# A decoder block with a chunked recurrence: its preparation divided by token halves and spread between the bursts of the recurrence

## The chip, the cores and the metric

One core of a Trainium2 chip (trn2) runs the kernel. The time is device microseconds of one launch. Engines are named as in the profile: PE (matmul), PEld (its weight loads), DVE, ACT, POOL, SP (which issues the DMAs).

## The reference, cut to what matters

Three layers, each `x = layernorm(x + layer(x))`, on x of 16 x 64 tokens x 256 features:

```python
# 1: recurrence with a state per head (16 heads of 16), 16 sequences of 64 tokens in chunks of 16
q = silu(x @ Wq); k = normalise(x @ Wk); v = x @ Wv; beta = sigmoid(x @ Wbeta) * 2
def step(S, (qi, ki, vi, ei)):
    kh = ki @ S;  kh_hat = layernorm(kh)
    gw = (w * kh_hat + b - (vi - ki)) * w
    v_new = (gw - mean(gw) - kh_hat * mean(gw * kh_hat)) * rstd
    qh = qi @ S - (tril(qi @ ki.T) * ei) @ v_new
    o = qi + layernorm(qh) * w + b
    S = S - (ki * ei).T @ v_new
o = rmsnorm(o * sigmoid(x @ Wg1 @ Wg2)) * norm_w @ Wo
# 2: cross attention to ctx (16 x 64 x 128), 16 heads of 128, rmsnorm on q and k
# 3: feed-forward (704), input, weights w1, w2 and hidden rounded to 127 levels (quant-dequant)
```

Each of the 16 sequences has 64 tokens, so the recurrence has `NCH` = 4 chunks, and all sequences and heads go through a chunk together.

## The kernel before, in words

It is written by hand for each engine: every engine has its own list of work, in order, and semaphores between them. The order of an engine's list is all that decides what runs when.

**Preparation** is a list of `jobs`: each fills one of the eight PSUM banks in turn (job n takes bank n % 8) on PE and is emptied by ACT or DVE (`emptied_by`). In order: four jobs transpose x (`xt`); k, q, v, four jobs of four passes each (L446); beta (L453), gate (L461); transposes of ctx and of the value weights; the row scales of w1 (`s1`, through a matrix `diag`); transposes of the rounded w1; `mvo`, value weights times output weights (L501); then `s2` and `w2t`. DVE turns k and v into rows (L1115, L1126), squares and normalises k, and rounds w1 and w2 (L1087); POOL scales w1 and w2, makes `diag`, and adds and multiplies the bias and weight of the inner norm into `pR` (`p_rows`, L1459).

**Recurrence.** For each chunk c and each half h (features), PE runs three kinds of bursts of 64 small tiles: `scores_ttt(c, h)` (L554), `state_products(c, h)` (L562) and `own_terms(c, h)` (L572). DVE reads the state product and sums its squares (`state_read`), ACT takes the root, DVE works through `chain(c, h)` (L1201 to L1221) to `ub`, which `own_terms` wants, then reads the result and updates the state (`after_own_terms`, L1231 to L1239), which the next chunk's `state_products` want. The output of a chunk is normalised, gated and normalised again: ACT squares (L914, L918), DVE sums and inverts (L1244, L1248), POOL gates it in four operations (`out_gated`, L1482 to L1486) and scales it (L1490); the last chunk is done by DVE.

In the gaps between the bursts stand the 32 **key units** of the cross attention, placed by `KEY_PLACES`: a projection (L535), a square and a copy on ACT (L896, L900), and a column sum (L525). All of chunk 0's bursts come after all preparation jobs.

**Token pipeline.** From `ttt_out(0)` (L723) on, eight tiles of 128 tokens go through output projection, attention and feed-forward. It wants x again, and the four quarters of Wq of the cross attention (`xwq`), whose buffers lie over data of the recurrence: SP loads quarter 0 and x in chunk 1's time, 1 and 2 in chunk 2's, 3 after the last burst.

Of the kernel before, what the change touches and what calls it, by code (L numbers as in the profile page):

```python
# [23 lines left out]

# [11 lines left out]
P = 128  # L36
# [18 lines left out]
KEY_PLACES = [(2, 1, 2, 2, 1), (1, 2, 1, 1, 2, 1), (1, 2, 1, 1, 2, 1), (1, 2, 3, 2)]  # L55
# [3 lines left out]
def decoder_block(nc, x, ctx_in, Wq, Wk, Wv, Wo, Wbeta, ln_w, ln_b, Wg1, Wg2, norm_w,  # L59
                  XWq, XWk, XWv, XWo, gq, gk, w1_in, w2_in, out):  # L60
    stack = ExitStack()
    with stack:
# [31 lines left out]
        ctx2 = place("ctx2", B * CD)  # L94
        mvo = place("mvo", XH * D)
        w1t = place("w1t", KT * FF, BF16)
# [13 lines left out]
        xwv = place("xwv", XH * XD)  # L110
        xwo = place("xwo", XH * D)
        assert cursor[0] <= kt_at + 6 * XH * P

        cursor[0] = kt_at + 6 * XH * P
        xt = place("xt", KT * B * T)
        xwvt = place("xwvt", XH * CD)
        assert cursor[0] <= after_kt
# [8 lines left out]
        xwk = place("xwk", XH * XD)  # L126
        ctxt = place("ctxt", B * T)
        krow1 = place("krow1", BANK, over="ctxt")
        pR = place("pR", NCH * CW)
        onehot = place("onehot", 64)  # L130
        kinv = place("kinv", P)
        qbR = place("qbR", NCH * CW)
        sgR = place("sgR", NCH * CW)
        negeta = place("negeta", NCH * G)
        wR, bR, w2R = (place(n, KT * 32) for n in ("wR", "bR", "w2R"))
        nwc = place("nwc", KT * 32)
        chain_at = cursor[0]

        kR = place("kR", NCH * CW)
        tmp1 = place("tmp1", NCH * CW, over="ogt")  # L140
        wk, wq, wv = (place(n, KT * D) for n in ("wk", "wq", "wv"))
        wbeta = place("wbeta", KT * H)
        wbg = place("wbg", KT * P)
        wg1 = place("wg1", KT * DH)
        wg2 = place("wg2", D)
        bgt = place("bgt", B * T)
        ss = place("ss", NCH * G)
        sd = place("sd", NCH * G)
        diag = place("diag", NW1 * P)
        w2q = place("w2q", KT * FF // 2, BF16)  # L150
        prelim_end = cursor[0]
# [9 lines left out]
        sup = place("sup", CW)  # L161
        m12 = place("m12", 2 * G)
# [4 lines left out]
        cursor[0] = max(cursor[0], prelim_end)  # L167
# [3 lines left out]
        ksq = place("ksq", 2 * BANK)  # L171

# [80 lines left out]
        for n in range(4):  # L253
            job("xt", n, by="act" if n < 2 else "dve")
        for kind, by in (("k", "dve"), ("q", "act"), ("v", "dve")):
            for hh in range(KT):
                for half in range(2):
                    job(kind, hh, half, by=by)
        for half in range(2):
            job("beta", half, by="act")  # L260
        for hh in range(KT):
            for half in range(2):
                job("gate", hh, half, by="act")
        for n in range(2):
            job("ctxt", n, by="act")
        for n in range(4):
            job("xwvt", n, by="act")
        for n in range(3):
            job("s1", n, by="act")
        for n in range(4):  # L270
            job("w1t", n, by="act")
        for n in range(8):
            job("mvo", n, by="act")
        job("s2", 0, by="act")
        for n in range(2):
            job("w2t", n, by="act")
        index_of = {(k, key): n for n, (k, key, _) in enumerate(jobs)}

        def emptied_by(n):
            by = jobs[n][2]  # L280
            return sem("prep_" + by), sum(1 for j in jobs[:n + 1] if j[2] == by)

# [39 lines left out]
        def _(sp):  # L322
# [3 lines left out]
            def load_x():  # L326
                flat = x.rearrange("b t d -> (b t) d")
                for half in range(2):
                    load(xn[:, half * 4 * D:(half + 1) * 4 * D].rearrange("p (i d) -> p i d", d=D),
                         flat[half * 512:(half + 1) * 512, :].rearrange("(i p) d -> p i d", p=P), "x")  # L330
# [18 lines left out]
            for k in range(KT):  # L349
                load(nwc[:, k:k + 1], norm_w.rearrange("(k p o) -> k p o", p=P, o=1)[k], "nw")  # L350
# [1207 lines left out]
```

## Time and profile before

| | us |
|---|---|
| median of 3 runs | 446.63 |
| the three runs | 441.91, 446.63, 449.75 |
| profiled execution | 441.95 |
| its span, first to last instruction | 440.1 |

| engine | busy us | share of span |
|---|---|---|
| PE | 362.4 | 82% |
| DVE | 266.0 | 60% |
| ACT | 218.0 | 50% |
| POOL | 120.9 | 27% |

The busy shares are averages over stages that have different limits; the windows by stage and the chain of waits say more. The granted clock of PE over the span is 0.919 of the full 2.4 GHz; it has two levels, so this is a mix of stretches at 1.2 and at 2.4.

### The profile page before, as it was taken

Reading aid. Unit: us, or ns where it says so; the run is one execution under the profiler, and the core shown is the slowest. Engines: PE = TensorE matmul, PEld = TensorE weight load, DVE = VectorE, ACT = ScalarE, POOL = GpSimd, SP = SyncE. Lnnn points to the kernel's source line nnn. Section 1 sums busy time; section 2 is a strip of 40 time slices with the busy share of each in tenths; the row PEclk is TensorE's granted clock in tenths of the full one; section 3 lists DMA queues with packets and bytes.
Section 4 is the critical chain, followed back from the end, with each engine's and each line's share of the span. In section 5 each row is a group of like instructions: output and inputs, shape, how many; then the busy total and the mean of one; then the engine's idle time right before and its main releaser. Section 6 shows DMA issues by size and latency. Waiting matters only on the chain.

```text
span 440.1 us, 10666 instructions
## 1 busy us (share of the span) xinstructions
PE 362.4 (82%) x4506; PEld 212.4 (48%) x4506; DVE 266.0 (60%) x494; ACT 218.0 (50%) x584; POOL 120.9 (27%) x132
## 2 busy tenths in 40 slices
PE   3999979779977735596799999999999999996942
PEld 2445844435433212343465665755757557473621
DVE  1579945499996886504243384673946728367564
ACT  3035954545533333063646757468475584753320
POOL 3042891022040041103033332343223432233001
PEclk9999969988968969589899999999999999998975
DMA  8990000000323001901010010100100100000000
GB/s 260 240 365 11 1 4 5 3 4 3 81 75 101 2 0 35 211 7 48 0 41 11 1 48 12 44 6 13 49 12 25 25 14 0 12 3 0 12 0 25
DMA packets 17630, 19.93 MB, mean 45 GB/s; under 512 B 3360, under 2 KB 15024, under 8 KB 17328
## 3 DMA queue, kind: packets, MB, share of 16 engines
q1 hardware_dynamic: 17552, 19.24, 16.0%
q8 instruction: 36, 0.59, 0.6%
q14 instruction: 10, 0.08, 0.1%
q10 hardware_dynamic: 32, 0.02, 0.0%
HBM read 18.07 MB, written 1.18 MB: 44 GB/s over the span
## 4 chain that ended last, share of the span: by engine, by line
PE 50%; DVE 19%; ACT 13%; POOL 8%; issue 7%; DMA 1%; SPq 1%; POOLq 0%; DVEq 0%; ACTq 0%
PE ps L626 9%; PE ps L535 7%; PE ps L672 5%; PE ps L446 5%; PE ps L525 4%; PE ps L680 3%; PE ps L640 3%; PE ps L572 3%; POOL pr L1525 3%; POOL pr L1527 3%; PE ps L554 3%; PE ps L649 2%; DVE pr L1382 2%; DVE pr L1379 2%; DVE mx L1381 2%
## 5 line engine op out<-in xcount | busy, mean ns | idle before, releaser
L626 PE MATMUL ps<-xwq,x1t 128*128 128x512 f32 x128 | 65.0, 638 | 0.9 <-ACT x1t L997 0.9
L680 PE MATMUL ps<-mvo,cxp 128*128 128x256 f32 x256 | 58.4, 382 | 0.1
L680 PEld LDWEIGHTS ps<-mvo,cxp 128*128 128x128 f32 x256 | 47.6, 190 | 6.7 <-issue 0.4
L535 PE MATMUL ps<-ctxt,xwk 128*128 128x512 f32 x64 | 39.0, 716 | 2.4 <-issue 2.2
L975 ACT ACTIVATE qjunk<-ps 128x128 f32<-128x128 f32 x128 | 33.5, 280 | 9.9 <-PE ps L626 9.7
L896 ACT ACTIVATE ksq<-ps 128x512 f32<-128x512 f32 x32 | 19.0, 594 | 38.3 <-PE ps L525 28.2
L626 PEld LDWEIGHTS ps<-xwq,x1t 128*128 128x128 f32 x128 | 24.0, 202 | 27.5 <-issue 24.7
L985 ACT ACTIVATE qt<-ps 128x512 f32<-128x512 f32 x32 | 19.2, 601 | 23.4 <-PE ps L640 23.3
L525 PE MATMUL ps<-ksq,onehot 128*32 128x512 f32 x64 | 21.8, 680 | 9.2 <-ACT ksq L896 9.1
L672 PE MATMUL ps<-pt,ctx 64*128 64x512 f32 x64 | 28.0, 657 | 0.2 <-ACT cxp L1006 0.2
L975 ACT ACTIVATION_READ_ACCUMULATOR qjunk<-ps 128x1 f32 x128 | 27.1, 212 | 0.0
L1525 POOL TENSOR_TENSOR pr<-pr,rq 128x1024 f32<-128x1024 f32 x7 | 13.3, 1901 | 49.1 <-DVE pr L1382 49.1
L1355 DVE TENSOR_TENSOR rr<-ps,xn 128x256 f32<-128x256 f32 x8 | 3.4, 424 | 34.6 <-PE ps L723 34.5
L1362 DVE TENSOR_TENSOR gs<-ps,s 128x352 f32<-128x352 f32 x16 | 8.4, 525 | 25.1 <-PE ps L699 25.1
L1519 POOL TENSOR_TENSOR rq<-rq,mhalf 128x16 f32<-128x16 f32 x8 | 23.3, 2909 | 0.7
L640 PEld LDWEIGHTS ps<-ident,qtok 128*128 128x128 f32 x128 | 15.3, 141 | 16.1 <-issue 12.8
L1508 POOL TENSOR_SCALAR rstd<-mv 128x1 f32<-128x1 f32 x24 | 5.3, 219 | 61.5 <-DVE mv L1318 61.5
L900 ACT ACTIVATE kt<-ps,gks 128x512 f32<-128x512 f32 x32 | 21.8, 682 | 0.0
L1006 ACT ACTIVATE cxp<-ps 128x512 f32<-128x512 f32 x32 | 18.9, 627 | 5.1 <-PE ps L672 5.1
L640 PE MATMUL ps<-ident,qtok 128*128 128x128 f32 x128 | 19.7, 277 | 0.9 <-ACT qtok L976 0.9
L997 ACT ACTIVATE x1t<-ps 128x256 f32<-128x256 f32 x8 | 3.1, 383 | 34.7 <-PE ps L731 34.7
L1323 DVE TENSOR_SCALAR x<-rr,mv,rstd 128x256 f32<-128x256 f32 x16 | 6.6, 413 | 22.5 <-POOL rstd L1509 22.5
(212 smaller groups left out, 736.5 us busy)
## 6 DMA issues: line engine op xcount, KB each, us to landing
rkb<-kscale SPq DMA_DIRECT2D x16, 256.0 KB, 4.0
xn<-in_x_dram SPq DMA_DIRECT2D x4, 512.0 KB, 5.4
ctx<-in_ctx_dram SPq DMA_DIRECT2D x4, 512.0 KB, 8.7
xwo<-in_L_xattn_Wo_dram SPq DMA_DIRECT2D x1, 2048.0 KB, 14.2
xwq<-in_L_xattn_Wq_dram SPq DMA_DIRECT2D x4, 512.0 KB, 5.4
w1n<-in_L_ffn_w_gate_up_dram SPq DMA_DIRECT2D x1, 1408.0 KB, 8.9
xwv<-in_L_xattn_Wv_dram SPq DMA_DIRECT2D x1, 1024.0 KB, 11.0
xwk<-in_L_xattn_Wk_dram SPq DMA_DIRECT2D x1, 1024.0 KB, 16.5
```

The lines of the kernel that those rows point to most:

```text
L446: last = mm(bank(bk), w[:, k * D + hh * P:k * D + (hh + 1) * P], xt[:, k * B * T + half * BANK:k * B * T + (half + 1) * BANK], start=k == ...
L525: mm(bank(5)[rows, :], onehot[:, at:at + 32], ksq[:, (n % 2) * BANK:(n % 2 + 1) * BANK], start=h < 2, stop=h >= XH - 2).then_inc(sem("k_su ...
L535: mm(bank(6 + n % 2), xwk[:, h * XD:(h + 1) * XD], ctxt[:, half * BANK:(half + 1) * BANK], start=True, stop=True)\
L626: last = mm(bank(n % 2), x1t[:, (i % 2) * D + k * P:(i % 2) * D + (k + 1) * P], xwq[qn][:, k * BANK:(k + 1) * BANK], start=k == 0, stop=k ...
L640: last = nc.tensor.transpose(bank(bk, P, t * P), qtok[:, (n % 2) * BANK + t * P:(n % 2) * BANK + (t + 1) * P], ident[:, :])
L672: turn_done(mm(bank(bk), ctx2[rows, b * CD:(b + 1) * CD], pt[rows, :].rearrange("p (h q) -> p h q", q=P)[:, :, b2 * T:(b2 + 1) * T], start ...
L680: last = mm(bank(6 + turn_of[("y", i, 0)] % 2, D), cxp[:, h * P:(h + 1) * P], mvo[:, h * D:(h + 1) * D], start=h == 0, stop=h == XH - 1)
L900: A(o, bank(6 + n % 2).rearrange("p (i t) -> p i t", t=P), ACT.Copy, scale=gks[:, 1:2]).then_inc(sem("key_emptied"), 1)
L975: A(qjunk[:, t * P:(t + 1) * P], bank(n % 2, P, t * P), ACT.Square, accum_out=qraw_ss[:, h:h + 1])
L985: ins = A(qt[:, n * BANK:(n + 1) * BANK], src, ACT.Copy)
L1519: GP.tensor_tensor(rq[:, :], rq[:, :], mhalf[:, :], ALU.pow).then_inc(sem("rq_ready"), 1)
L1525: GP.tensor_tensor(groups(z, T), groups(z, T), spread(rq[:, :], XH, T), ALU.mult).then_inc(sem("z_ready"), 1)
```

## The change

- Jobs have banks of their own choice (`BANKS`): those of the second half of the tokens, and all later ones, go round banks 5, 6, 7, since the recurrence holds 0 to 4.
- x is loaded and transposed in another token order (`load_tokens`), so that half 0 holds chunks 0 and 1, and half 1 chunks 2 and 3. k, v, beta of half 0 and q are prepared first; chunk 0 begins then. The rest of the preparation stands between the bursts of chunks 0 to 2, the key units behind it, in chunks 2 and 3 and after the last burst (`KEY_TAIL`).
- POOL does nothing in the recurrence. ACT scales w1 and w2 and makes `diag` (26 instructions), folds weight and bias into v when it copies it, adds the bias to q (`q_biased`), and squares k and the state products. DVE makes `pR` (`p_rows`) and gates and scales the output (`gated`, `scaled`).
- The mask of the scores is applied by halves. xwk is loaded when `k_feat` is at 2. SP loads all of `xwq` and x after the last burst, behind `scales_out(0)`.

The diff, cut to its core:

```diff
-        for n in range(4):
-            job("xt", n, by="act" if n < 2 else "dve")
+        in_bank(0, "xt", 0, 0, by="act")
+        in_bank(1, "xt", 1, 0, by="dve")
+        in_bank(4, "k", 0, 0, by="dve")
...
+        ring = itertools.cycle((5, 6, 7))
+        in_bank(next(ring), "q", 1, 1, by="act")
+        for hh in range(KT):
+            in_bank(next(ring), "v", hh, 1, by="act")
...
+        for kind, count in (("ctxt", 2), ("xwvt", 4), ("mvo", 8), ("s1", 3), ("w1t", 4), ("s2", 1), ("w2t", 2)):
+            for n in range(count):
+                in_bank(next(ring), kind, n, by="act")
...
# SP
-            load_x()
+            load_tokens(0)
+            load_weight(wk, Wk, "wk")
+            load_weight(wv, Wv, "wv")
+            load_weight(wbeta, Wbeta, "wb")
+            load_weight(wg1, Wg1, "wg")
+            load_tokens(1)
+            load_weight(wq, Wq, "wq")
...
-            load(xwk[:, :], XWk, "xwk")
+            sp.wait_ge(sem("k_feat"), 2)
+            load(xwk[:, :], XWk, "xwk")
...
             roots_to_rows(0)
-            sp.wait_ge(sem("mg_done"), 2 * 2)
-            load_xwq(0)
-            load_x()
             scales_out(0)
-            sp.wait_ge(sem("og_ready"), 2)
-            load_xwq(1)
-            load_xwq(2)
+            sp.wait_ge(sem("mg_done"), 2 * NCH)
+            load_x(0)
+            for qn in range(4):
+                load_xwq(qn)
+            load_x(1)
             roots_to_rows(1)
-            sp.wait_ge(sem("mg_done"), 2 * NCH)
-            load_xwq(3)
# PE: its order
+            x_transposes(0, 0)
+            x_transposes(1, 0)
+            projection("k", 0, 0)
+            projection("k", 1, 0)
+            x_transposes(0, 1)
+            x_transposes(1, 1)
+            projection("v", 0, 0)
+            projection("v", 1, 0)
+            beta(0)
+            projection("q", 0, 0)
+            projection("q", 1, 0)
+            projection("q", 0, 1)
             scores_ttt(0, 0)
+            projection("q", 1, 1)
             scores_ttt(0, 1)
+            projection("v", 0, 1)
+            own_terms(0, 0)
+            projection("v", 1, 1)
+            scores_ttt(1, 0)
+            beta(1)
+            gate(0, 0)
+            own_terms(0, 1)
+            gate(0, 1)
+            gate(1, 0)
+            gate(1, 1)
+            projection("k", 0, 1)
+            projection("k", 1, 1)
+
+            state_products(1, 0)
+            ctx_transposes(0)
+            ctx_transposes(1)
+            state_products(1, 1)
...
+            own_terms(1, 0)
+            value_out(1)
+            value_out(2)
+            scores_ttt(2, 0)
...
+            own_terms(2, 0)
+            w2_transposes(0)
+            w2_transposes(1)
+            keys(2)
+            scores_ttt(3, 0)
+            keys(3)
+            own_terms(2, 1)
+            keys(4)
+
+            state_products(3, 0)
+            keys(3)
+            state_products(3, 1)
+            keys(3)
+            scores_ttt(3, 1)
+            keys(3)
+            own_terms(3, 0)
+            keys(5)
+            own_terms(3, 1)
+            keys(sum(KEY_TAIL) + 1)
# PE: key_unit(0)
                     pe.wait_ge(sem("ld_xwk"), 16)
+                    for by in ("act", "dve"):
+                        pe.wait_ge(sem("prep_" + by), sum(1 for j in jobs if j[2] == by))
# ACT: chunks 1 and 3
+            output_square(0)
+            state_square(1, 0)
+            k_square(1)
+            ctx_out(0)
+            ctx_out(1)
+            state_root(1, 0)
+            w1_scaled()
+            state_square(1, 1)
...
+            state_root(3, 1)
+            keys(3)
+            gated_square(2)
+            keys(5)
+            output_root(6)
# DVE: chunk 1, and the end of 2
+            state_read(1, 0)
+            kb_rows(1)
+            k_rows(1)
+            state_sums(1, 0)
+            step_sizes(1)
+            dve.wait_ge(sem("w2_rows"), 1)
+            chain(1, 0)
+            state_read(1, 1)
+            output_sums(1)
+            k_sums(1)
+            state_sums(1, 1)
+            a_masked(1, 1)
+            k_normalised(1)
+            output_inverse(1)
+            chain(1, 1)
+            p_rows(1)
+            gate_rows()
+            q_rows()
...
+            gated(0)
+            after_own_terms(1, 0)
+            output_sums(2)
+            a_masked(2, 0)
+            after_own_terms(1, 1)
+            output_inverse(2)
+            scaled(0)
+            weights_rounded("w1")
+            weights_scale("w2")
...
+            chain(2, 1)
+            weights_rounded("w2")
+            gated(1)
+            after_own_terms(2, 0)
# POOL: all of its work in the recurrence goes
-            def out_gated(c):
...
-            for c in range(NCH - 1):
-                out_gated(c)
-                out_scaled(c)
```

## Rows read from the trace of the kernel before

**Rows 1.** Windows by stage: busy microseconds (instructions) by engine, PEclk, DMA share, GB/s.

```profile
0.00:56.00 56.00, 46.40 (x186) 27.56 (x186) 36.98 (x35) 26.58 (x49) 21.33 (x31) 1.00 0.60 172
56.00:80.00 24.00, 21.86 (x906) 12.55 (x908) 11.47 (x25) 12.03 (x24) 11.07 (x9) 0.86 0.02 4
80.00:109.00 29.00, 23.52 (x778) 11.55 (x766) 23.18 (x50) 13.32 (x25) 5.04 (x4) 0.88 0.02 4
109.00:140.00 31.00, 23.50 (x837) 12.32 (x827) 27.22 (x57) 14.24 (x28) 7.15 (x6) 0.89 0.30 91
140.00:171.00 31.00, 21.29 (x487) 8.13 (x479) 22.84 (x51) 11.02 (x22) 5.55 (x5) 0.84 0.01 3
...
179.00:440.00 261.00, 225.60 (x1376) 140.10 (x1376) 137.51 (x267) 139.81 (x438) 69.90 (x78) 0.93 0.09 23
```

**Rows 2.** Chain of work that ended last: start, microseconds, what.

```profile
11.78 20.85 PE ps L446 x48
...
68.08 1.19 PE ps L554 x86
69.27 1.92 PE ps L535 x4
71.19 0.98 PE ps L525 x4
...
76.56 1.49 PE ps L572 x128
...
178.80 2.09 PE ps L723 x4
```

**Rows 3.** Timeline of DVE: start, duration, line, operation, idle before and releaser.

```profile
97.58 1.37 DVE L1203 TENSOR_TENSOR gwx<-xh,w2R 128x256 f32<-128x256 f32 x1
...
105.56 0.44 DVE L1231 STREAM_TRANSPOSE qhR<-ps 128x256 f32<-128x256 f32 x1
...
107.51 0.69 DVE L1244 TENSOR_REDUCE ovs<-osq 128x32 f32<-128x512 f32 x1
...
112.20 1.24 DVE L1160 STREAM_TRANSPOSE ak<-kb 128x1024 f32<-128x1024 f32 x1
...
114.61 0.25 DVE L1201 RECIPROCAL rs<-sdc 128x16 f32<-128x16 f32 x1
...
115.36 0.43 DVE L1203 TENSOR_TENSOR gwx<-xh,w2R 128x256 f32<-128x256 f32 x1
...
120.50 0.45 DVE L1178 STREAM_TRANSPOSE khR<-ps 128x256 f32<-128x256 f32 x1
```

**Rows 4.** Timeline of PE, with the same columns.

```profile
6.44 3.65 PE L435 MATMUL ps<-ident,xn 128*128 128x128 f32 x16 [6.44 <-DMA xn<-in_x_dram]
...
93.03 0.31 PE L554 MATMUL ps<-kq,kb 32*32 32x16 f32 x15 [1.66 <-issue]
...
96.76 0.41 PE L554 MATMUL ps<-kq,kb 32*32 32x16 f32 x17 [1.32 <-issue]
...
118.50 1.13 PE L535 MATMUL ps<-ctxt,xwk 128*128 128x512 f32 x2
...
123.79 0.92 PE L554 MATMUL ps<-kq,kb 32*32 32x16 f32 x50 [3.39 <-issue]
124.64 2.08 PE L535 MATMUL ps<-ctxt,xwk 128*128 128x512 f32 x2
...
160.67 1.92 PE L525 MATMUL ps<-ksq,onehot 128*32 128x512 f32 x2 [9.08 <-ACT ksq L896]
```

**Rows 5.** Window with the first late transfers in it, columns as in the first group.

```profile
121.00:124.00 3.00, 0.21 (x16) 0.21 (x20) 2.54 (x6) 1.51 (x4) 0.72 (x1) 0.78 0.79 268
```

**Rows 6.** Page, its part on DMA queues: packets, MB, share.

```profile
q8 instruction: 36, 0.59, 0.6%
```

**Rows 7.** Timeline of ACT in the last chunk.

```profile
159.50 0.63 ACT L918 ACTIVATE osq<-oR 128x512 f32<-128x512 f32 x1 [5.56 <-POOL oR L1486]
```

**Rows 8.** Lines: busy, mean ns, idle before.

```profile
L1087 DVE TENSOR_SCALAR w1q<-w1n 128x2816 bf16<-128x2816 f32 x1 | 1.6, 1629 | 0.0
```

More of the change, by code:

```diff
@@ L25 @@
+import itertools
 from contextlib import ExitStack
@@ L131, in decoder_block @@
         kinv = place("kinv", P)
+        ss = place("ss", NCH * G, over="kinv")
         qbR = place("qbR", NCH * CW)
@@ L161, in decoder_block @@
         sup = place("sup", CW)
+        wv = place("wv", KT * D, over="sup")
         m12 = place("m12", 2 * G)
@@ L449, in _ @@
-            pe.wait_ge(sem("wbg_ready"), 2 * KT)
-            for half in range(2):
+                for k in range(KT):
+                    wait(emptied_by(index_of[("xt", (k, half))]))
+                bk = open_job(kind, hh, half)
+                for k in range(KT):
+                    last = mm(bank(bk), w[:, k * D + hh * P:k * D + (hh + 1) * P],
+                              xt[:, k * B * T + half * BANK:k * B * T + (half + 1) * BANK], start=k == 0, stop=k == KT - 1)
+                done(last)
@@ L451, in _, with beta @@
+            def beta(half):
+                pe.wait_ge(sem("wbg_ready"), 2 * KT)
                 bk = open_job("beta", half)
@@ new lines, in _ @@
+            act.wait_ge(sem("consts"), 2)
+            k_square(0)
+            x_out(0, 1)
+            k_root(0)
+            v_out(0, 0)
+            v_out(1, 0)
+            beta_out(0)
+            act.wait_ge(sem("masks"), 2)
+            act.wait_ge(sem("k_feat"), 1)
+            k_blocks(0)
+            q_out(0, 0)
+            q_out(1, 0)
+            q_out(0, 1)
+            q_out(1, 1)
+            v_out(0, 1)
+            k_blocks(1)
+            v_out(1, 1)
+            beta_out(1)
@@ new lines, in _ @@
+            q_biased()
+            act.wait_ge(sem("k_feat"), 2)
+            k_blocks(2)
+            value_out(0)
+            value_out(1)
+            value_out(2)
+            value_out(3)
+            value_out(4)
+            gated_square(0)
+            w1_diagonals()
+            output_root(2)
+            value_out(5)
+            value_out(6)
+            value_out(7)
+            output_square(1)
+            state_square(2, 0)
+            s1_out(0)
+            s1_out(1)
+            s1_out(2)
@@ new lines, in _ @@
+            state_root(2, 0)
+            w2_scaled()
+            w2_diagonals()
+            state_square(2, 1)
+            output_root(3)
+            state_root(2, 1)
+            w1_out(0)
+            w1_out(1)
+            k_blocks(3)
+            w1_out(2)
+            w1_out(3)
+            s2_out()
+            gains_and_wo()
+            w2_out()
+            keys(2)
+            gated_square(1)
+            keys(3)
+            output_root(4)
+            keys(4)
+            output_square(2)
@@ new lines, in _ @@
+            V.tensor_reduce(tri[:, :], kb[:, P:2 * P].rearrange("p (j w) -> p w j", w=C), AX.X, ALU.add).then_inc(sem("masks"), 1)
+            x_out(1, 1)
+            k_sums(0)
+            k_normalised(0)
+            p_rows(0)
+            step_sizes(0)
+            dve.wait_ge(sem("masks"), 2)
+            chain(0, 0)
+            kb_rows(0)
+            a_masked(0, 0)
+            chain(0, 1)
+            a_masked(0, 1)
+            after_own_terms(0, 0)
+            a_masked(1, 0)
+            after_own_terms(0, 1)
```

729 lines of the change are left out of this document (388 added, 341 removed).

## Prediction

> **What bounds the kernel now.** I began with the windows by stage [rows 1], cut where the recurrence's chunks begin. Up to 56 us lies the preparation, from 56 to 171 us the four chunks of the recurrence with the key projections in their gaps, then an 8 us tail that only DVE works on, and from 179 us the token pipeline. The reader is to see two things. The last stage, 261 us of the 440.1, is touched by nothing in the diff but its first moments, so the question is when `ttt_out(0)` starts: 178.80 us in the chain of waits [rows 2]. And ahead of it no engine is full: PE is busy 46, 22, 24, 24 and 21 us of stages of 56, 24, 29, 31 and 31 us, DVE 37, 11, 23, 27 and 23.
>
> The chain of waits gives the price of each kind of PE work: 48 passes of projections in 20.85 us, so 0.434 us a pass and 1.74 us a job of four; a burst of the recurrence (64 small tiles) 1.2 us for scores and 1.5 us for own terms; two key projections 1.92 us and their two sums 0.98 us, so 1.45 us a key unit [rows 2]. The timelines show three losses:
> - DVE's operations on two SBUF tensors take 1.37 us while POOL gates (97.58) and 0.43 us when it doesn't (115.36) [rows 3]. Four of them in the second half of each of three chunks: 3 x 4 x 0.9 = about 11 us.
> - PE stands with nothing to wait for inside bursts: 1.66, 1.32 and 3.39 us [rows 4]. A burst is 64 tiles, two passes each, with a weight load for each pass: 256 instructions. The page counts 36 packets and 0.59 MB on the instruction queue, 16 KB a packet [rows 6], so I read the stalls as PE waiting for its program. The two resume points at 93.03 and 96.76 lie 3.7 us apart: bursts closer together than that must wait. The 3.39 us stall falls in a window in which 268 GB/s of data came in [rows 5], so I take 5.7 us a packet under load.
> - After such a stall and after the 9.08 us in which PE waits at the last chunk, the granted clock in the window is below 1, and two key passes take 2.08 us where they took 1.13 [rows 4]. That wait is ACT standing at `gated_square` for POOL's gating [rows 7].
>
> **The change, part by part.** Everything is split at token half, the recurrence begins when the first half is ready, and the rest is spread over the chunks. This turns the time to the pipeline into four pieces, each with one engine that sets it. I work each from durations.
>
> *A, PE sets it, from its first projection to the first state product.* Before, PE begins at 6.44 us, when 1 MB of x has landed, and projects from 11.78 us [rows 2, 4]. Now 0.5 MB is wanted first, and DVE's copy no longer stands behind the beta weights. I estimate the first transposes at 5.0 us (two SP issues more, half the bytes), two jobs at 3.65/4 = 0.91 us [rows 4] and a copy of 0.7 us: 7.5 us. In front of `state_products(1, 0)` stand 12 projections and 2 beta jobs (14 x 1.74 = 24.3), 4 gate jobs of two passes (3.5), 2 x transposes (1.8), 3 score bursts (3.7) and 2 own-term bursts (3.0), then that burst itself (1.25). With 1.7 us of waits for ACT (the SiLU of q stands behind two table loads and `k_blocks`) this is 39.3 us: 46.8 us. The five bursts in it lie 3 us apart with one projection between, while the weight loads still run to about 30 us (1.5 MB fewer than before up to there). By the packet times above I take 2 us at the first, 2.7 at the second, 0.7 at each of the next two, and 0.9 us for a slow spell: 7 us. Bounds: 0, if packets are ahead, and 14 us, if every burst stalls 2.8. So 53.8 us.
>
> *B, DVE sets it, from the first state read to w2 rounded.* An operation costs 0.43, 0.69 and 1.24 us at 256, 512 and 1024 elements [rows 3], so about 2.3 at 2048 and 3.1 at 2816; a `chain` 5.9 us (114.61 to 120.50) and an `after_own_terms` 1.95 us (105.56 to 107.51) [rows 3]. Chunk 1 now holds 2 chains (11.8), 2 after (3.9), `kb_rows`, state reads, sums, inverses and masks (5.9), k rows, sums and normalising (5.7), `p_rows` (3.0), step sizes (0.9), gate and q rows (4.6), the gating that was POOL's (4 x 0.73 = 2.9), scaling and transpose (1.4), w1 rounding (1.6 [rows 8]) and the scale of w2 (2.0): 43.7 us, plus 2.4 us for `state_root(1, 0)`, which stands on ACT behind the k square, two copies and a table load. Chunk 2 up to the rounding of w2: 2 chains and 6.0 us: 17.8. Together 63.9 us, where chunks 1 and 2 took 29 and 31 us before. The 11 us of the port are saved, but gating (8.7 us over three chunks) and 22 us of preparation come on DVE. PE has some 9 us of slack in chunk 1, so stalls there cost nothing. 53.8 + 63.9 = 117.7.
>
> *C, the hand-over.* `key_unit(0)` now waits for every preparation job, the last of which is w2: transposes 0.95 us (bf16, estimated from 12 small passes) and ACT's three copies 1.6: 120.2 us.
>
> *D, PE sets it again.* All 32 key units stand behind that: 46.4 us, with seven bursts (9.0). DVE's second half of chunk 3 no longer suffers from POOL but gates itself, and ACT still stands at `gated_square(2)` with two units unevacuated: where PE waited 9.08 us I get 5.0. Slow spells: one at the start, after PE has waited for w2, and one behind that wait; two to three key units at double price each, 4.9 us. The last root 0.7. Sum 66.0: the pipeline starts at 186.2. DVE's tail (about 13 us) lies beside the last ten units (14 us) and costs nothing; if those weren't there it would be the bound.
>
> *Edges of the pipeline.* PE is at work up to its start, so I take 2 us back from the first projections of q, which ran at the lower clock (0 to 4). SP now issues x and all of Wq, 3 MB, after the last own terms and behind `scales_out(0)`, which waits for DVE's `key_scales(0)`: some 3 us after the last burst, then 3.0 MB / 268 GB/s [rows 5] = 11.7 us and 2 us of landing. That ends within 1 us of the first use. The w1 and w2 scaling and the diagonals go from POOL to ACT in 26 instructions of an estimated 0.4 us: 10 us that lie beside DVE's 64. SP now waits for `k_feat` before it loads xwk (1 MB, 4 us at 268 GB/s [rows 5]), some 75 us in; behind it on SP stands only `roots_to_rows(0)`, due after 120 us, when xwk is first used too: nothing.
>
> Sum: 186.2 - 178.8 = +7.4, less 2 = +5.4 us. The profiled execution took 441.95 us, so 447.3; **I say 447 us**. The three runs have a median of 446.63, and 441.95 is near their lowest (441.91); against the median the sum would read 452, and I leave the difference in the range.
>
> On the packets the Trainium skill speaks the other way: Runtime: NRT & Kernel Launch, Instruction fetch mechanics, has the program streamed in 16 KiB blocks, the crossing of a block mostly hidden. By that the 7 us of piece A would be nothing and the time 440. The trace doesn't agree, with 1.32 to 3.39 us inside bursts [rows 4].
>
> **The rivals.**
> 1. *My sum*, within about 2% of before. For it: gains and losses are on different engines but in series. Chance 0.47.
> 2. *PE never starves, clearly faster.* Program packets come in time because other work lies between bursts (piece A 7 us shorter), and so the clock stays at its upper level in D (4.9 us), and ACT reaches `gated_square(2)` when it is ready (5.0). 447 - 17 = 430 us. For it: before, bursts with 3 to 4 us between them at 68 to 77 us show no stall at all [rows 2]. Against: PE must wait for w2 at C anyway. It decides from 14 us saved of the 17. Chance 0.28.
> 3. *The clock falls in piece A, slower.* The bursts are small tiles, and in the stage where they first appear the granted clock is 0.86 [rows 1]. If the wide jobs between the bursts ran at half speed, six projections (10.4) and four gates (3.5) would double: 447 + 14 = 461 us. It decides from 4 us on, a third of these jobs. Against: in the windows up to 56 us the clock is 1.00 through dense projections. Chance 0.25.
> 4. *The late loads* are the wait that takes the place of others: with half the rate (a window of the recurrence shows far less than 268 GB/s on average, 91 [rows 1]) they would land 10 us late: 457 us. This is one way into the slower case, and its chance is in that of 3.
> 5. *The contention was no loss on the path.* Then POOL's idleness brings nothing: it is already off the path in my sum save in D, and the time stays 447.
>
> **How the numbers follow.** 447 is the likeliest case. The range reaches to rival 2's price and nearly to rival 3's: 431 to 461 us; the likeliest case's own range is 439 to 456. About 2% is what the measurement can tell. Faster by more than 2%: 0.27, within: 0.48, slower: 0.25.
>
> **What would show each step.** A: the first state product near 54 us, with stalls inside the five bursts; right if they sum to some 7 us. B: DVE busy over 90% for 60 us, its two-tensor operations at 0.43 us everywhere, w2's rounding near 118 us. C and D: the first key projection near 120 us, a wait of PE of about 5 us before the last own terms, `ttt_out(0)` at 186 us, and x and Wq landed just by then. From there 261 us less two. The prediction is wrong if DVE shows gaps in chunk 1 (then PE or ACT's order sets it), if the first key unit comes before 110 us, or if the pipeline itself changes its length by more than 4 us.

## The result, and the profile of the changed kernel

The changed kernel takes 448.88 us (median of four runs, 448.79 to 449.63), the kernel before 445.00 (four runs, 441.91 to 449.75): a ratio of 1.0105, 95% interval 1.006 to 1.015. That is a slowing of about 1%, inside the 2% of which the prediction speaks. The profiled execution took 448.79 us with a span of 446.9; that of before 441.95 with 440.1. Run beside the later kernels, the kernel before had medians of 445.8 to 446.7. Its profiled execution is one of its fastest, that of the changed kernel lies at its median, so that marks in the two traces differ by more (6.8 us at the end) than the medians do (2 to 4 us). The changed kernel, run again, has a median of 450.56 over six executions, three at 447.88 to 448.04 with a mean granted clock of 0.913 to 0.917, three at 453.08 to 454.37 with 0.902 to 0.903.

Windows by stage of the changed kernel, cut at the four pieces of the prediction (columns as in [rows 1]):

```profile
0.00:54.80 54.80, 44.47 (x849) 23.34 (x850) 25.07 (x52) 21.95 (x34) 4.21 (x23) 0.97 0.54 148
54.80:88.00 33.20, 22.48 (x704) 18.19 (x704) 29.55 (x60) 18.69 (x40) 0.00 (x0) 0.76 0.11 35
88.00:116.20 28.20, 14.98 (x542) 10.22 (x542) 26.51 (x61) 16.20 (x39) 0.00 (x0) 0.67 0.01 3
116.20:155.00 38.80, 36.95 (x821) 15.60 (x824) 21.46 (x50) 24.10 (x46) 0.00 (x0) 0.91 0.01 3
155.00:188.00 33.00, 27.73 (x237) 7.73 (x225) 16.77 (x33) 19.07 (x36) 0.00 (x0) 0.90 0.30 99
188.00:446.90 258.90, 223.00 (x1376) 138.68 (x1376) 137.55 (x267) 140.19 (x438) 69.93 (x78) 0.94 0.11 26
```

The alternation is plain: from 54.8 to 116.2 us DVE is busy 56.1 of 61.4 us and PE 37.5; from 116.2 to 155 PE is busy 36.95 of 38.8. In [rows 1] PE had 69 to 91% of a stage of the recurrence and DVE 48 to 88%, in each stage both. Now one engine at a time is full, and the full ones stand in series: `ttt_out(0)` starts at 187.94 us instead of 178.80. The granted clock of 0.76 and 0.67 in the two windows of DVE is PE's, which has time there. The pipeline behind `ttt_out(0)` takes 259.0 instead of 261.3 us.

Timeline of PE of the changed kernel, at the places where it loses time:

```profile
5.36 1.94 PE L466 MATMUL ps<-ident,xn 128*128 128x128 f32 x8 [5.36 <-DMA xn<-in_x_dram]
8.18 6.68 PE L476 MATMUL ps<-xt,wk 128*128 128x512 f32 x8 [0.88 <-DVE xt L1313]
...
27.31 1.25 PE L595 MATMUL ps<-kq,kb 32*32 32x16 f32 x128
...
33.96 1.02 PE L595 MATMUL ps<-kq,kb 32*32 32x16 f32 x94 [3.06 <-issue]
34.91 3.56 PE L476 MATMUL ps<-xt,wv 128*128 128x512 f32 x4
...
53.47 1.29 PE L603 MATMUL ps<-kq,st 32*32 32x32 f32 x128
...
116.26 1.30 PE L548 MATMUL ps<-ident_b,w2q 128*128 128x128 bf16 x12 [2.22 <-DVE w2q L1308]
118.56 3.75 PE L570 MATMUL ps<-ctxt,xwk 128*128 128x512 f32 x4 [0.99 <-issue]
...
162.13 2.08 PE L570 MATMUL ps<-ctxt,xwk 128*128 128x512 f32 x2 [3.62 <-ACT kt L1042]
164.13 1.92 PE L558 MATMUL ps<-ksq,onehot 128*32 128x512 f32 x4
...
182.11 1.12 PE L570 MATMUL ps<-ctxt,xwk 128*128 128x512 f32 x2 [0.26 <-ACT kt L1042]
...
187.94 1.97 PE L822 MATMUL ps<-wo,ogt 128*128 128x256 f32 x8 [0.86 <-ACT krow L1029]
```

L476 are the projections, L595 the scores, L603 the state products, L570 and L558 a key unit's projection and sums. Of the stalls inside bursts of [rows 4] one large one is left (3.06 us at 33.96), beside 1.51 us at 60.45 and 1.07 us at 103.17. In three places the passes take about double: eight k passes in 6.68 us where the same eight take 3.6 us at 49.95, four v passes in 3.56 us behind the stall, and four key passes in 3.75 us, which take 1.98 later. The windows of these three (columns as above):

```profile
8.18:14.80 6.62, 6.62 (x9) 2.74 (x10) 1.20 (x4) 0.00 (x0) 0.71 (x3) 1.00 0.72 171
34.91:38.40 3.49, 3.49 (x8) 1.17 (x4) 3.23 (x12) 0.00 (x0) 0.00 (x0) 0.54 0.02 5
118.56:122.30 3.74, 3.74 (x8) 1.20 (x12) 2.19 (x4) 1.18 (x2) 0.00 (x0) 0.50 0.02 4
```

The second and third lie at the lower level of the granted clock (0.54 and 0.50). The first shows 1.00 although its passes take as long as those of the others, so there only the durations speak of a slower PE.

Timeline of DVE, its gating of chunk 0 and the start of the second chain of chunk 2:

```profile
88.65 0.69 DVE L1507 TENSOR_TENSOR oR<-oR,sgR 128x512 f32<-128x512 f32 x1
...
110.18 0.42 DVE L1438 TENSOR_TENSOR gwx<-xh,w2R 128x256 f32<-128x256 f32 x1
...
115.32 0.89 DVE L1308 TENSOR_SCALAR w2q<-w2n 128x1408 bf16<-128x1408 f32 x1
```

The operation that took 1.37 us beside POOL (97.58 in [rows 3]) takes 0.42, with POOL idle (0.00 in every window from 54.8 to 188 us).

### The profile page after: what moved, and what is told of

It is laid out like the page before. It is cut to its first block, busy times and chain, and to the rows that moved or that the text cites. A ratio compares the mean times of both kernels' runs of the same rounds, so it can differ in the third digit from the quotient of the medians.

```text
span 446.9 us, 10762 instructions
## 1 busy us (share of the span) xinstructions
PE 369.6 (83%) x4506; PEld 213.8 (48%) x4506; DVE 256.9 (57%) x519; ACT 240.2 (54%) x632; POOL 74.1 (17%) x101
## 4 chain that ended last, share of the span: by engine, by line
PE 36%; DVE 23%; ACT 10%; POOL 6%; issue 5%; POOLq 0%; DVEq 0%; ACTq 0%
PE ps L725 8%; PE ps L570 5%; PE ps L771 5%; PE ps L779 3%; PE ps L558 3%; PE ps L739 3%; POOL pr L1785 3%; POOL pr L1787 3%; PE ps L748 2%; DVE pr L1694 2%; DVE pr L1691 2%; DVE sm L1705 2%; DVE mx L1693 2%; ACT pr L1230 2%; ACT sg L1235 2%
## 5 line engine op out<-in xcount | busy, mean ns | idle before, releaser
L725 PE MATMUL ps<-xwq,x1t 128*128 128x512 f32 x128 | 63.5, 623 | 1.2 <-ACT x1t L1216 0.9
L570 PE MATMUL ps<-ctxt,xwk 128*128 128x512 f32 x64 | 38.0, 695 | 6.2 <-ACT kt L1042 5.2
L725 PEld LDWEIGHTS ps<-xwq,x1t 128*128 128x128 f32 x128 | 23.0, 194 | 26.3 <-issue 23.6
L570 PEld LDWEIGHTS ps<-ctxt,xwk 128*128 128x128 f32 x64 | 11.0, 206 | 26.5 <-ACT kt L1042 15.2
L748 PE MATMUL ps<-ident,pr 128*128 128x128 f32 x64 | 10.5, 316 | 12.3 <-POOL pr L1787 6.7
```

Source lines behind the costliest of these rows:

```text
L570: mm(bank(6 + n % 2), xwk[:, h * XD:(h + 1) * XD], ctxt[:, half * BANK:(half + 1) * BANK], start=True, stop=True)\
L725: last = mm(bank(n % 2), x1t[:, (i % 2) * D + k * P:(i % 2) * D + (k + 1) * P], xwq[qn][:, k * BANK:(k + 1) * BANK], start=k == 0, stop=k ...
L748: last = nc.tensor.transpose(bank(bk, P, t * P), pr[:, col:col + P], ident[:, :])
```

## The experiments

Unless said otherwise each starts from the changed kernel. "First key unit" and "`ttt_out(0)`" are starts on PE in the profiled execution; the changed kernel has 118.56 and 187.94, and its first state product at 53.47.

### Which engine sets which piece

Two kernels carry the same superfluous operation on DVE, a repeat of the maxima of w1 into an unused tile, 3.04 us. The one has it in piece B, the other in piece A.

```diff
             weights_scale("w2")
+            step(V.tensor_reduce(wsc2[:, 0:NW1], groups(w1n...), AX.X, ALU.max, ...))   # in B
```
```diff
+            dve.wait_ge(sem("ld_w1"), 16)
+            step(V.tensor_reduce(wsc2[:, 0:NW1], groups(w1n...), AX.X, ALU.max, ...))   # in A
             after_own_terms(0, 1)
```

> One more DVE operation of 3.04 us (the maxima of w1 once more, into an unused tile) behind the scale of w2, in piece B. Theory, DVE sets piece B: everything behind it moves by the whole of it, first key unit at 121.6 us where the changed kernel had 118.56, time 448.9 + 3.1 = 452.0 us. Rival, PE or ACT sets the chunks and DVE has room: less than 1 us, 449 to 450.

> The same 3.04 us operation on DVE in piece A, in front of after_own_terms(0, 1), where DVE stood 3.85 us for PE. Theory, PE sets piece A: the operation fills the wait and the time stays, 448.9 within 0.5 us. Rival, the path runs through DVE in chunk 0 too: +3 us, 452.

In B: 452.0 us (ratio to before 1.0116, 95% interval 1.002 to 1.0212; the others likewise), first key unit 121.76, `ttt_out(0)` 191.11, both 3.2 us later. In A: 448.58 us (1.0087, 1.0039 to 1.0135), first state product 53.08, first key unit 118.29: nothing. Here the k passes took 5.30 us and the first scores came at 25.78 instead of 27.31; of these 1.5 us 1.1 went again in slower passes behind the same stall (1.47, 3.78 and 2.04 us for 1.02, 3.56 and 1.56), with no wait of PE for DVE up to the state product. `ttt_out(0)` came at 189.83 in this profile, 1.9 us later than in the changed kernel, by passes at the lower clock at the start of D: that mark moves by 2 us without an edit in D. Timeline of PE of the kernel with it in B:

```profile
119.44 1.32 PE L549 MATMUL ps<-ident_b,w2q 128*128 128x128 bf16 x12 [2.23 <-DVE w2q L1309]
121.76 2.90 PE L571 MATMUL ps<-ctxt,xwk 128*128 128x512 f32 x3 [0.99 <-issue]
```

So DVE sets B, and doesn't set A.

### What sets piece A: PE's passes or its program

```diff
+            for n in range(12):
+                mm(bank(7, P), ident[:, :], ident[:, :], start=True, stop=True)
             x_transposes(0, 0)
             x_transposes(1, 0)
+            for n in range(3):
+                mm(bank(7, P), ident[:, :], ident[:, :], start=True, stop=True)
```

> Twelve throw-away matmuls of 128 columns on PE before x has landed and three more while its copies are made, so that PE is at work when the k projections come. Theory, the eight k passes took 6.68 us instead of 3.6 because the clock was at its lower level after idling: they fall to about 3.6, first state product 3 us earlier, time 446. Rival, piece A waits for the weights' landing or for DVE there: no change, 448.9.

448.01 us (1.0073, 1.0026 to 1.012), below the 448.88 of the changed kernel by less than its own spread. With PE at work from 2.5 us the k passes take 3.67 us, the first scores come at 24.70 instead of 27.31, and the first state product still at 53.22. Timeline of PE:

```profile
8.57 3.67 PE L476 MATMUL ps<-xt,wk 128*128 128x512 f32 x8 [0.21 <-DVE xt L1317]
...
31.21 1.21 PE L595 MATMUL ps<-kq,kb 32*32 32x16 f32 x123 [3.16 <-issue]
...
38.54 0.23 PE L616 MATMUL ps<-ak,ub 32*32 32x48 f32 x1 [1.06 <-issue]
...
42.57 0.25 PE L595 MATMUL ps<-kq,kb 32*32 32x16 f32 x7 [0.71 <-issue]
```

The 2.6 us won at the start are lost in three stalls, 4.93 us in sum instead of 3.06, and in slower passes. `ttt_out(0)` is at 185.91, but of these 2.0 us 1.7 arise in D, where nothing was edited. The next kernel takes the data traffic away from the bursts:

```diff
+            sp.wait_ge(sem("mg_done"), 1)
             load(xwv[:, :], XWv, "xwv")
             load(xwo...
```

> SP waits for the first own terms before it loads xwv and xwo (3 MB) and what stands behind them; the scores of chunk 0 then run with little other traffic. Theory, program packets come late because they share the DMA engines with the weight loads: the stall of 3.06 us inside scores_ttt(0, 1) shrinks to what stalls without traffic were, 1.3 to 1.7 us, or goes, first state product 2 us earlier, time 447 (448.9 before). Rival, the packet's own latency sets it: the stall stays at 3 us and nothing moves, 448.9, or the loads arrive late for value_out and move the stall there.

447.6 us (1.0063, 1.0023 to 1.0102). The stall in `scores_ttt(0, 1)` is gone, one of 2.20 us appears at 42.77 in `own_terms(0, 1)`, where these loads now run (344 GB/s from 40.6 to 42.8 us), and the first state product comes at 51.91, the first key unit at 117.54, `ttt_out(0)` at 184.30. In the changed kernel the window 25 to 31 us, ahead of the stall, has 349 GB/s; the one behind it, 35 to 40, has 7 GB/s and a clock of 0.69:

```profile
25.00:31.00 6.00, 5.83 (x172) 2.94 (x171) 4.62 (x14) 3.29 (x9) 0.00 (x0) 1.00 1.09 349
35.00:40.00 5.00, 5.00 (x133) 2.62 (x133) 3.31 (x12) 1.49 (x3) 0.00 (x0) 0.69 0.03 7
```

So the large stall follows the loads. What that is worth is less than the marks say. Of the 1.6 us at the first state product 1.1 were there at the first scores (26.21 instead of 27.31, the k passes having taken 5.66 us), and the kernel with this edit and two others, below, has its first state product at 52.78, the unchanged one run again at 53.07. Of the 3.6 us at `ttt_out(0)` 2.6 lie in D: the wait of 3.61 us is still there, but the passes behind it took 1.12 and 1.05 us instead of 2.08 and 1.92. Nothing in the edit accounts for that.

That the stalls are PE's program arriving is not read off a packet, but the traces hold more for it than the traffic does. The stall stands at one place of PE's list: behind 34 of the 128 matmul records of `scores_ttt(0, 1)` in all eight profiled executions without the throw-away matmuls and with the loads as they were, though PE came there at times up to 1.9 us apart. With the throw-away matmuls, 30 more records ahead (24 and 6), it stands behind 5, 29 records earlier. With the loads moved it stands behind 15 records of `own_terms(0, 1)`, and with loads moved and throw-away matmuls in (the last kernel below) behind 113 of them. Timeline of PE, the place in the changed kernel, in that with throw-away matmuls, and in that with later loads:

```profile
30.42 0.48 PE L595 MATMUL ps<-kq,kb 32*32 32x16 f32 x34
...
27.81 0.24 PE L595 MATMUL ps<-kq,kb 32*32 32x16 f32 x5
...
42.77 2.51 PE L617 MATMUL ps<-ak,ub 32*32 32x48 f32 x113 [2.20 <-issue]
```

The kernel before and its variant with DVE's gating, below, share such places too, with 17, 50 and 67 records of a burst left (at 96.76, 123.79 and 139.78 us in the one, at 96.15, 130.18 and 144.85 in the other). A place that goes with the count of instructions and not with the time fits a program fetched in blocks of fixed size; loads beside it make the wait longer.

### What gating on DVE and POOL's idleness are worth

The kernel before with the gating moved to DVE (four operations and the scaling per chunk, the same as in the change), nothing else changed:

```diff
-            for c in range(NCH - 1):
-                out_gated(c)
-                out_scaled(c)
# DVE, chunk c: gated(c - 1) where it waited for POOL's first, scaled(c - 1) behind output_inverse(2 * c)
```

> The kernel before with one part of the change alone: the gating and scaling of chunks 0 to 2 on DVE instead of POOL, in the same places. Theory of exchange: each chunk saves 3.7 us of operations slowed to 1.37 us and pays 4 x 0.73 + 0.7 = 3.6 us, and DVE no longer slows at chunk 3, where PE waited 9.08 us for the gating: that wait shrinks by about 2, time within 3 us of before (444 to 447). Rival, the port cost before its full 11 us on the path: time 436. Second rival, DVE has no room: each chunk longer, 450.

448.64 us (1.0061, 1.0017 to 1.0106), 1.9 us above the median of the kernel before beside it, and `ttt_out(0)` at 186.76 where the kernel before had 178.80. The even exchange that I expected is not there, although DVE has no operation of 1.37 us left in chunks 2 and 3: DVE's own gating costs the kernel before more than POOL's did, contention included. PE waits longer, not shorter, in the last chunk (it was 9.08 us in [rows 4]):

```profile
167.54 1.91 PE L525 MATMUL ps<-ksq,onehot 128*32 128x512 f32 x2 [11.82 <-ACT ksq L896]
```

The other way round, the changed kernel with gating and scaling back on POOL:

```diff
-            gated(0)
+            dve.wait_ge(sem("qh_used"), 1)
-            scaled(0)
+            out_c(0)
# and so for chunks 1 and 2; POOL: out_gated(c), out_scaled(c) as before
```

> The changed kernel with that part undone: POOL gates and scales chunks 0 to 2. Theory: in chunk 1 DVE gives up 3.6 us of work and waits about 1.5 for POOL; in chunk 2 and 3 the gating falls beside chain(c, 1), whose four operations go from 0.43 to 1.37 us. B ends at about 118 us instead of 116.2, PE's wait in D stays near 4 us: time 449 to 452. Rival, DVE's length is all that counts and POOL works for nothing: 3 x 3.6 = 11 us off, 438.

450.14 us (1.0084, 1.0048 to 1.0119), 1.3 us above the changed kernel's median, which is within the spread of the two. Timelines of DVE, then of POOL:

```profile
111.70 1.27 DVE L1437 TENSOR_TENSOR xh<-khR,rs 128x256 f32<-128x256 f32 x1
113.01 1.38 DVE L1438 TENSOR_TENSOR gwx<-xh,w2R 128x256 f32<-128x256 f32 x1
114.42 1.37 DVE L1440 TENSOR_TENSOR gwx<-gwx,pR 128x256 f32<-128x256 f32 x1
115.82 1.37 DVE L1441 TENSOR_TENSOR gwx<-gwx,xh 128x256 f32<-128x256 f32 x1
...
118.03 0.42 DVE L1444 SCALAR_TENSOR_TENSOR dd<-m,gwx 128x256 f32<-128x256 f32 x1
```

```profile
111.64 1.06 POOL L1768 TENSOR_TENSOR oR<-qhR,ors 128x512 f32<-128x512 f32 x1 [14.47 <-DVE ors L1483]
...
115.59 1.33 POOL L1772 TENSOR_TENSOR oR<-oR,sgR 128x512 f32<-128x512 f32 x1
```

The four operations of DVE that run while POOL's four run take 1.27 to 1.38 us, the later ones 0.42. w2 is rounded at 121.87 instead of 116.21, 5.7 us late. DVE loses 4.8 us in B to slowed operations (3.7 in these four, 1.1 in the state update at 88.57) and 5.0 us to waits for POOL and for what hangs on it (1.40, 1.89, 0.57 and 1.17), and saves 3.6 us of gating and scaling. The first key unit comes at 124.52, 6 us late, yet `ttt_out(0)` at 188.48, only 0.5 late. D is shorter by 5.4 us, because POOL's gated output of chunk 2 is ready at 163.09, 2.7 us later than DVE's was (ACT squares it at 160.38), while PE comes there 6 us later: the wait of 3.62 us is one of 0.37, and no slow passes follow. So the contention is real and costs B about as much as the waits for POOL do, and the wait in D hides the sum. That the time came out as expected is luck: B was to end at 118 and the wait to stay near 4 us. What POOL's idleness would be worth in a kernel without that wait, no run tests.

### The wait in the last chunk, and the pace behind it

```diff
-            gated_square(2)
             keys(5)
+            gated_square(2)
             output_root(6)
```

> ACT does gated_square(2) behind the five key units instead of in front of them. Theory, PE sets piece D and the wait of ACT for DVE's gating stops it: PE's wait of 3.62 us ahead of the last own terms goes, and with it the slow spell behind it (162 to 168 us, where two key passes took 2.08 us, about 3 us lost): -6 us, 443. Rival 1, only the wait counts and the clock does not follow: -3.6, 445. Rival 2, DVE's tail takes over as bound: less than -2, 447 or more.

446.42 us (1.0004, 0.9966 to 1.0042), 2.5 us less than the changed kernel. The 3.62 us wait and the slow passes behind it are gone, and the last own terms come at 166.28 instead of 169.78, `ttt_out(0)` at 184.44. Timeline of PE:

```profile
159.43 1.13 PE L570 MATMUL ps<-ctxt,xwk 128*128 128x512 f32 x2
160.82 1.13 PE L570 MATMUL ps<-ctxt,xwk 128*128 128x512 f32 x2 [0.26 <-ACT kt L1042]
161.88 1.05 PE L558 MATMUL ps<-ksq,onehot 128*32 128x512 f32 x4
```

I had expected 6 us, and 3.5 came at `ttt_out(0)`; 2 of the missing went to a longer slow stretch at the beginning of D (own terms (2, 1) at 131.39 instead of 129.34). The 0.26 us waits that remain are the pace: a projection waits for ACT to empty its bank, and a pair of units takes 3.43 us (175.26 to 178.68 in the changed kernel). A third bank for the key units from 22 on:

```diff
+        def key_bank(n):
+            return 6 + n % 2 if n < 22 else (6, 7, 4)[(n - 22) % 3]
# PE: from unit 25 on, wait for key_emptied at n - 2; unit 24 doesn't wait
```

> Key units from 22 on go round three banks of PSUM (6, 7 and 4) instead of two, so a projection no longer waits for the copy of the unit but one. Theory, D is PE's only while ACT keeps up: in the tail a pair of units took 3.43 us where PE's own work is 2.9, with waits of 0.26 us shown and sums held up; five pairs give 2.0 to 2.5 us, time 446.5. Rival, DVE's tail (171 to 185 us) or the last square and root set it: less than 0.7, 448.5.

447.96 us (1.0052, 1.0015 to 1.0089), last own terms at 169.32 and `ttt_out(0)` at 185.89: 16.6 us between them instead of 18.2. Timeline of PE, where the pair is now down to 2.90 us (173.41 to 176.31):

```profile
173.41 1.98 PE L575 MATMUL ps<-ctxt,xwk 128*128 128x512 f32 x4
175.32 1.05 PE L561 MATMUL ps<-ksq,onehot 128*32 128x512 f32 x4
176.31 1.98 PE L575 MATMUL ps<-ctxt,xwk 128*128 128x512 f32 x4
```

### The hand-over, and the slow passes behind it

```diff
+            weights_rounded("w2")
             chain(2, 1)
-            weights_rounded("w2")
```

> The changed kernel with the rounding of w2 moved from behind chain(2, 1) to ahead of it on DVE; nothing else. It tests the hand-over: if the 2.2 us wait of PE for w2 is on the path and the slow first four key passes (3.75 us against 1.98) come from that wait, the first key unit comes at 116.4, its four passes take 2 us, own_terms(2, 1) no later than before, ttt_out(0) 3 to 4 us earlier, median -2 to -3 us. The rival: what PE does 2 us sooner it waits for later (DVE's chain ends 0.9 us later, ACT's gated squares), and the median moves by under 1 us; or the spell comes anyway, from the small tiles of own_terms(2, 0), and only 2 us are won.

446.35 us (1.0041, 0.9994 to 1.0088). Eight of its twelve executions took 445.06 to 447.54, against 447.88 to 448.04 for the three faster ones of the unchanged kernel run beside it. PE doesn't wait for w2, the first key unit comes at 116.07, and the four key passes take 1.96 us instead of 3.75:

```profile
113.81 0.96 PE L548 MATMUL ps<-ident_b,w2q 128*128 128x128 bf16 x12
116.07 1.96 PE L570 MATMUL ps<-ctxt,xwk 128*128 128x512 f32 x4 [1.30 <-issue]
```

`ttt_out(0)` comes at 184.94. The first key unit and this mark are both 2.4 us before those of the unchanged kernel run beside it, so D has the same length; of the expected 3 to 4 us the slow passes gave 1.8, and two stalls inside bursts, 0.87 and 0.82 us, took back as much. The unchanged kernel:

> The changed kernel with nothing edited, to have it beside the others in one call: 448.9 (448.4 to 449.6), first state product 54.8, first key unit 118.6, ttt_out(0) 187.9, each within 1 us.

First state product 53.07, first key unit 118.46, `ttt_out(0)` 187.38. The marks repeat within 0.6 us, at `ttt_out(0)` by chance, since two kernels whose first key units come at 118.29 and 118.26 have it at 189.83 and 185.91 (the expected 54.8 was the first read of DVE, not the product).

### Together

Squares behind the keys, later loads and the third bank in one kernel; then with the throw-away matmuls and the earlier rounding as well.

> Three earlier edits together: gated_square(2) behind keys(5), xwv and xwo loaded behind chunk 0, key units from 22 on round three banks. Alone they moved ttt_out(0) by -3.5, -3.6 and -2.1 us, in medians by -2.5, -1.3 and -0.9 us. If the pieces are in series, as my theory has it (A set by the arrival of PE's program under load, D by PE's waits and the spells behind them), the terms add: first state product near 52, ttt_out(0) near 180 to 181, median near 444 (442.5 to 446). The rival: another engine's list stands close behind PE's (DVE in the last chunk), so that less than 3 us of the 9 come through and the median stays at 446 or above.

> The three edits of the run before, and two more: throw-away matmuls at the start, and the rounding of w2 ahead of chain(2, 1) on DVE. If PE's start sets piece A as soon as the loads no longer collide with the bursts, the first state product comes at 50 to 51; if packets still set it, at 52. With w2 rounded earlier the first key unit should come 2 us sooner and without a slow spell behind it: ttt_out(0) near 176 to 178, median 441 (439 to 443). The rival: the clock or the packets take it back and it equals the run before within 1 us.

Three edits: **441.55 us** (0.993, 0.9893 to 0.9967), `ttt_out(0)` at 181.34, span 439.5; this is the fastest, and with the next the only one that is below the kernel before with its whole interval, by less than 1%. Five edits: 442.03 us (0.9956, 0.9918 to 0.9995), `ttt_out(0)` at 180.12. The three terms alone were -3.5, -3.6 and -2.1 us at `ttt_out(0)`; together -6.6. The 2.6 us that are missing are the slow passes in D, which were away in the kernel with later loads too and can't go twice. With three edits the first key unit comes at 118.13, 0.3 us before that of the unchanged kernel run beside it (118.46), and `ttt_out(0)` 6.0 before: nearly all of the gain lies in D, from the square behind the keys and the third bank, and the later loads have hardly a part in it. A kernel with those two edits alone wasn't run. The two others bring 1.2 us more at `ttt_out(0)` and nothing in the median, and neither mark came where I expected it (50 to 52 and 176 to 178). Timeline of PE with five edits: stalls of 2.14 and 2.78 us in own terms (0, 0) and (0, 1), first state product at 54.27, and the key passes slow again, though PE comes to w2 without a wait (transposes of w2 from 115.88, own terms until then). So the wait for w2 alone isn't the cause of the slow passes behind it.

```profile
35.76 0.23 PE L622 MATMUL ps<-ak,ub 32*32 32x48 f32 x1 [2.14 <-issue]
...
47.76 0.37 PE L622 MATMUL ps<-ak,ub 32*32 32x48 f32 x15 [2.78 <-issue]
...
118.14 3.58 PE L576 MATMUL ps<-ctxt,xwk 128*128 128x512 f32 x4 [1.30 <-issue]
```

## Why the prediction was right, step by step

The gain of the change is real and stands in its first line: the first scores begin at 27.31 us instead of 56.16. It is given back because the preparation that was taken out of the front, and the gating that was POOL's, go on DVE's list in B, and the key units, which filled PE's gaps before, all come behind B. The forecast of 447 us (447.3 in the sum) lies 1.9 below the measured 448.88, and 1.5 to 1.8 below the profiled 448.79, the number that the sum was made for. The four pieces and the engine of each are as predicted. That the end fits to 2 us is in part luck: inside and between the pieces +3.9, -2.1, -2.5 and +3.4 us cancel, and the sum starts at 441.95, the profiled execution, where from the median it would have read 452.

**A** (first state read on DVE: 53.8 predicted, 54.80 measured). The end is right and two terms in it are wrong in opposite directions. The k passes began at 8.18 instead of 7.5 and took 6.68 us where I had reckoned 3.5 at full speed: +3.9. The stalls and the slow spell, put at 7 us, were 3.06 and 1.8 (four v passes in 3.56 instead of 1.74): -2.1. The wait ahead of q was 0.97 instead of 1.7: -0.7. The throw-away matmuls show that the end hardly depends on this split: the 2.6 us that PE gains at the start it loses again, 1.9 in stalls and the rest in slower passes. In the kernels whose loads and start were left alone the first state product lies between 53.03 and 53.56, with first scores between 25.78 and 27.71. My model of the packets had too many stalls (five bursts, one stall), but what sets A is, as it said, more than PE's passes.

**B** (63.9, 61.4). The list of DVE's operations was sound, 2.5 us too long in sum; the wait for `sdc` was 2.65 against 2.4, and one of 0.61 us follows at 101.75. The stalls of PE in B, 1.51 and 1.07 us, lie in its slack (it waits 7.30 us for DVE at 91.23) and cost nothing, as predicted. The superfluous operation confirms the mechanism: 3.04 us in B cost 3.2.

**C** (2.5, 2.4). Right in sum; its parts were transposes of 1.30 us and 0.99 us in which PE waits for nothing that the profile shows.

**D** (66.0, 69.4). The wait at the gated square was 3.62 us instead of 5.0. Slow stretches cost 2.3 us at the start (3.75 for 1.98 and 1.71 for 1.24) and 2.7 behind the wait (2.08, 1.92 and 2.88 for 1.13, 1.05 and 1.98): 5.0 against 4.9. The term that was mis-sized is the key unit: I took 1.45 us from a pair in which nothing waited [rows 2], while six pairs of D waited for ACT at 3.43 instead of 2.90 us, 3.2 us in all. Of the 1.5 us left, 0.8 lie in the last four sums (1.86 instead of 1.05); the rest is not assigned.

**The pipeline** (-2, -2.3): right in its cause, which was worth twice that at first. Before, the first output projection ran in 3.78 us at a granted clock of 0.50 and the first twelve passes of q in 8.28 us at 0.65; now they take 1.97 and 5.87 us at 1.00. Timeline of PE before, then of the changed kernel:

```profile
185.16 8.28 PE L626 MATMUL ps<-xwq,x1t 128*128 128x512 f32 x12 [0.47 <-ACT x1t L997]
...
192.71 3.70 PE L725 MATMUL ps<-xwq,x1t 128*128 128x512 f32 x8 [0.47 <-ACT x1t L1216]
196.63 1.95 PE L725 MATMUL ps<-xwq,x1t 128*128 128x512 f32 x4 [0.22 <-ACT qtok L1195]
```

The scores of the first tile start 16.78 us behind `ttt_out(0)` instead of 20.77, a gain of 4.0. Four passes of q behind the next wait take back 1.1 (3.62 us at 218.65 against 2.56 at 213.49). The late loads were issued from 174.10 to 177.56 and came in at 179 and 218 GB/s in the windows 172 to 180 and 180 to 188; the first addition of x follows PE directly at 189.14, so they are hidden, as the sum had it.

**The rivals.** "PE never starves" fell: it needed 14 us, and the removable part of stalls, wait and pace, with three edits at once, was 7.3 us of median. Its terms in D were real, though, which is why the kernel with three edits is faster than before. "The clock falls in A" was to decide from 4 us on, by the wide jobs between the bursts: of these only four v passes ran at the lower level, for 1.8 us. The 3.2 us of the k passes lie ahead of the first burst, which no rival had, and at a granted clock of 1.00. "The late loads" fell. "The contention was no loss" is nearly right for the end of this kernel (0.5 us at `ttt_out(0)`, 1.3 of median) and wrong for B (4.8 us of slowed operations), and it holds at the end only because a wait in D hides it.

The Trainium skill, Runtime: NRT & Kernel Launch, Instruction fetch mechanics, has the crossing of a 16 KiB block of the program mostly hidden. The runs agree for most of the program, where bursts run through, and not where loads run beside it: 3.06 us here, gone from that burst when the loads were moved, 3.39 before and 4.41 in the kernel before with DVE's gating. Nor is it always so without loads: 2.17 us at 82.52 before and 2.06 at 105.99 with five edits, both with 0 GB/s in the window of the stall.

## What to carry to other kernels

When work is spread over stages, write down for each stage which engine will be full, and add the stages: two engines that take turns near 90% give little overlap, however idle each looks on average. A superfluous operation of known length is a cheap test of which engine sets a stage. A small wait in a list that otherwise runs full (an ACT operation two places too early, 3.6 us) costs itself and, in most profiles, slow passes behind it; three repairs together were worth 7.3 us, more than the whole rearrangement had lost. And before a gain at a late mark is put down to an edit, look where it arose: the later loads seemed to bring 3.6 us, of which 2.6 lay in a stretch that the edit doesn't touch.

## What the runs showed of the hardware

- PE's first eight k passes, behind a first wait of 5.2 to 6.0 us and 0.88 us more, took 5.30 to 6.68 us in ten profiled executions, and 3.67 us in both with throw-away matmuls from 2.5 us on. The granted clock of that stretch is 1.00 in all of them, so the row of the clock doesn't show this loss. In the kernel before the sixteen at 11.78 us took 7.11, full speed, behind more transposes.
- A slow stretch isn't tied to one wait: after a wait of 2.22 us for w2 four key passes took 3.75 us; with no wait there they took 1.96, but with five edits, where PE doesn't wait for w2 either, 3.58 again. And behind the wait of 3.6 us in D two key passes took 2.08 us in the changed kernel, 1.12 with throw-away matmuls, with slower ones only behind them, and 1.12 with later loads, with none slow at all. What decides it is open.
- Stalls in which PE waits for nothing that the profile shows stand at fixed places of its list (behind 34 of 128 records in eight profiled executions, behind 5 when 30 records were put ahead), and were up to 2.44 us long with no data coming in, 2.20 to 4.41 us with 190 to 370 GB/s in or just ahead of them.
- The last stretch of the pipeline, where nothing was changed, took 64.2 us at a clock of 0.74 in the profiled execution of the third-bank kernel (451.83 us, where its median is 447.96) and 59.0 at 0.80 in that of the changed kernel; both stretches begin 200 us behind `ttt_out(0)` (windows of the one, then of the other):

```profile
385.90:450.10 64.20, 45.37 (x232) 26.75 (x230) 33.13 (x69) 21.74 (x48) 10.86 (x15) 0.74 0.03 9
```

```profile
387.90:446.90 59.00, 39.61 (x228) 24.65 (x226) 32.68 (x68) 20.26 (x41) 10.79 (x14) 0.80 0.03 10
```

So a mark ahead of that stretch tells edits apart better than the median does. `ttt_out(0)` itself moves by 2 us with the clock in D, and the mark next behind the edit is better still.
